# Two transformer layers on one core: q and k as two scaled fp16 parts in the two 64-row halves of the array

## What is computed

```python
x = x + _L0_attn_ref(_layernorm(x), ...)   # 16 heads of 16 dims, biases, ALiBi slopes, causal
x = x + _L0_ffn_ref(_layernorm(x), ...)    # hidden 704, int32 weights minus 128 times a scale
x = x + _L1_attn_ref(_layernorm(x), ...)   # 16 heads of 16 dims, no bias, causal
x = x + _L1_ffn_ref(_layernorm(x), ...)    # hidden 768, weights rounded to fp8
# attention, per head (layer 0 has alibi and biases):
attn = jnp.einsum('bhqd,bhkd->bhqk', q, k) / jnp.sqrt(jnp.float32(D)) + alibi
p = jax.nn.softmax(jnp.where(causal, attn, jnp.finfo(jnp.float32).min), axis=-1)
o = jnp.einsum('bhqk,bhkd->bhqd', p, v)
```

## Time and profile before

| | |
|---|---|
| median of 3 runs | 438.41 us (436.98 to 442.74) |
| profiled execution, span | 441.7 us |
| TensorE busy | 410.0 us (93%) |
| VectorE busy | 297.1 us (67%) |
| ScalarE busy | 232.9 us (53%) |
| GpSimd busy | 170.2 us (39%) |
| attention, layer 0 / layer 1 | about 37 to 168 us / 259 to 388 us |

### The profile page before, as it was taken

The page is one execution under the profiler, slowest core; times in us unless marked ns, Lnnn a source line. Parts: engine busy times, 40 slices in busy tenths (PEclk is TensorE's granted clock), DMA queues, the critical chain, the costliest instruction groups (busy, mean ns, idle before and its releaser), DMA issues.

```text
span 441.7 us, 14528 instructions
## 1 busy us (share of the span) xinstructions
PE 410.0 (93%) x6328; PEld 237.2 (54%) x6328; DVE 297.1 (67%) x596; ACT 232.9 (53%) x377; POOL 170.2 (39%) x250
## 2 busy tenths in 40 slices
PE   5799789999999988999999998998999999888997
PEld 5356564555555347544377466544555553465476
DVE  4636489999998216521336586899999981188883
ACT  3535355577776973221101541655877769635950
POOL 4107013314033144478692000234361544453770
PEclk9989799999999999999999997999999999999999
DMA  6899550000000000200100479400000000000002
GB/s 204 129 239 263 128 148 4 4 3 4 4 2 5 4 1 6 65 8 9 64 0 0 120 200 224 106 5 4 3 4 3 4 5 2 2 1 0 1 26 71
DMA packets 21657, 22.97 MB, mean 52 GB/s; under 512 B 2588, under 2 KB 20858, under 8 KB 21594
## 3 DMA queue, kind: packets, MB, share of 16 engines
q1 hardware_dynamic: 20498, 19.03, 17.8%
q0 software_dynamic: 544, 2.49, 1.9%
q10 hardware_dynamic: 552, 0.53, 0.4%
HBM read 8.27 MB, written 1.05 MB: 21 GB/s over the span
## 4 chain that ended last, share of the span: by engine, by line
PE 71%; DVE 14%; ACT 4%; DMA 3%; issue 3%; POOL 2%; SPq 2%; ACTq 0%; DVEq 0%
PE ps L785 11%; PE ps L765 11%; DVE mx L1258 11%; PE ps L743 10%; PE ps L916 8%; PE ps L1012 5%; PE ps L944 4%; PE ps L921 4%; ACT prob L1141 4%; PE ps L677 4%; PE ps L980 4%; DMA col_rows<-in_L_ffn_up_scale 3%; PE ps L845 3%; PE ps L751 2%; POOL xn L605 1%
## 5 line engine op out<-in xcount | busy, mean ns | idle before, releaser
L1258 DVE TENSOR_REDUCE mx<-ps 128x1 f32<-128x512 f32 (+3 forms) x304 | 181.1, 654 | 28.9 <-PE ps L751 24.1
L1141 ACT ACTIVATE prob<-ps 128x1024 f32<-128x1024 f32 (+1 forms) x192 | 145.4, 812 | 63.4 <-PE ps L765 63.1
L743 PE MATMUL ps<-kS,qS 96*32 96x512 bf16 (+21 forms) x1536 | 111.9, 321 | 4.4 <-DVE mx L1258 3.0
L590 POOL TENSOR_SCALAR_AFFINE_SELECT prob<-prob 128x256 f32<-128x256 f32 x128 | 51.9, 412 | 163.9 <-ACT prob L1141 162.5
L765 PE MATMUL ps<-qS,kS 101*32 101x512 bf16 (+7 forms) x1536 | 95.2, 326 | 3.7 <-ACT prob L1141 3.6
L785 PE MATMUL ps<-prob,v 128*32 128x512 f32 (+3 forms) x768 | 80.1, 489 | 0.6 <-POOL prob L590 0.4
L743 PEld LDWEIGHTS ps<-kS,qS 99*32 99x32 bf16 (+1 forms) x1536 | 42.8, 95 | 50.4 <-DVE mx L1258 28.1
L748 PE MATMUL ps<-mask_q,identb 128*32 128x32 bf16 (+1 forms) x1024 | 51.1, 186 | 2.7 <-issue 2.7
L765 PEld LDWEIGHTS ps<-qS,kS 101*32 101x32 bf16 (+1 forms) x1536 | 35.0, 96 | 31.2 <-ACT prob L1141 15.8
L751 PE MATMUL ps<-mask_q,identb 128*32 128x64 bf16 (+1 forms) x512 | 45.4, 198 | 0.0
L748 PEld LDWEIGHTS ps<-mask_q,identb 128*32 128x32 bf16 x1024 | 28.1, 98 | 14.0 <-issue 9.2
(11 more groups left out here) (146 smaller groups left out, 537.0 us busy)
## 6 DMA issues: line engine op xcount, KB each, us to landing
qS<-parts SPq DMA_DIRECT2D x24, 128.0 KB, 3.3
kS<-parts SPq DMA_DIRECT2D x24, 128.0 KB, 3.4
qS<-prob SPq DMA_DIRECT2D x12, 128.0 KB, 8.0
kS<-prob SPq DMA_DIRECT2D x12, 128.0 KB, 7.5
qS<-xn SPq DMA_DIRECT2D x12, 128.0 KB, 3.4
kS<-xn SPq DMA_DIRECT2D x12, 128.0 KB, 2.9
out<-x SPq DMA_DIRECT2D x8, 128.0 KB, 1.7
oT<-in_L_ffn_gate_w POOLq DMA_DIRECT2D x1, 768.0 KB, 4.8
```

Of the source, the lines that this page charges most:

```text
L590: nc.gpsimd.affine_select(out=square, in_=square, compare_op=ALU.is_ge, fill=0.0, base=0, pattern=[[0, 2], [1, P]], channel_multiplier=-1) ...
L743: mmi = nc.tensor.matmul(span[r:r + STRIP, 0:seen], qS[0:K_MAX[L], c, g * G + h, qt * P + r:qt * P + r + STRIP], kS[0:K_MAX[L], g * G + h, ...
L1141: nc.scalar.activation(prob[:, n % 3, 2 * pair:2 * pair + 2, off:CH], ps[:, 2 * (m % 2):2 * (m % 2) + 2, off:CH], ACT.Exp, scale=SCALE).th ...
L1258: ins = nc.vector.tensor_reduce(mx[:, slot, qt, heads[0]:heads[-1] + 1, part], src, AX_X, ALU.max)
```

## The change

- q and k are split into two fp16 parts rather than three bf16 parts. Three products of parts remain (`Q_PARTS`, `K_PARTS`), 48 rows a head; with ALiBi and the maximum 53 rows at most. Even heads stand in partitions 0 to 63, odd heads in 64 to 127 (`rows_of`), and a product is addressed to a half of the array's rows and a strip of its columns: 64 x 32 rather than 128 x 32. `mid` and its copies fall away.
- fp16 has a small range, so q and k are first scaled by powers of two `sigma` (a bound on their size from the norm of the weights: a sum of squares on ScalarE, a product with a constant on TensorE, maximum and power on GpSimd, a mask of exponent bits on VectorE). The scale goes into the weights as they are turned; the exponential's scale becomes a value in memory per partition, `exp_scale`, and was a constant. The ALiBi rows need the inverse of the scale in `qS`, written by two broadcast transfers.
- The maxima go in pairs of items: the same queries of two neighbouring heads, one in each half of the rows, into two banks of the ring of three. A diagonal item holds at most two heads (was four), so a c = 0 group has 12 items and a c = 1 group 28, in 6 and 14 pairs. `ORDER` counts pairs.
- `qS` and `kS` have half as many columns; a job is still six transfers, now of 64 KB, and each maximum is two transfers. `parts` has a slot of its own for each job and `fT` its own memory.
- Layer 1's scale is a side job (`bound_w1`) ahead of the transposes of the down weights.

```diff
-Q_PARTS = (0, 0, 0, 1, 1, 2)
-K_PARTS = (2, 0, 1, 0, 1, 0)
+Q_PARTS = (0, 0, 1)
+K_PARTS = (0, 1, 0)
...
-T_LAG = 2
-TURN_AHEAD = 5
+T_LAG = 1
+TURN_AHEAD = 3
...
+        def rows_of(h, rows):
+
+            return slice(h % 2 * HALF, h % 2 * HALF + rows)
...
+                    if (L, k) == (0, 1):
+                        sp.wait_ge(unit_row_done, 1)
+                        for half in range(2):
...
+                            sp.dma_start(q_rows[rows], src).then_inc(tail_in, 16)
...
+            def scales(L, w):
...
+                    nc.gpsimd.tensor_scalar(floored[:, L, m:m + 1], norms[:, L, m:m + 1], NORM_FLOOR[m], None, ALU.max).then_inc(sigma_step, 1)
...
+                nc.gpsimd.tensor_tensor(roots[:, L, last], floored[:, L, last], nhalf[:, last], ALU.pow).then_inc(roots_done, 1)
...
+            def bound_w0(w):
+                bank = take_a(("norm", w))
+                pe.wait_ge(squared, w + 1)
+                nc.tensor.matmul(bank[:, 0:1], to_bound[:], row_sums[:, 0, w:w + 1], start=True, stop=False)
...
+            def bound_w1():
+                bank = take_a(("norms1",))
+                pe.wait_ge(squared, 4)
+                nc.tensor.matmul(bank[:, 0:2], to_bound[:], row_sums[:, 1, :], start=True, stop=True).then_inc(a_full, 1)
...
+            def max_scores(L, n, cg, pair):
                 g, c = CGS[cg]
-                qt, part, heads, key0, keys = item
-                bank = ps[:, 4 + n % M_BANKS]
-                for i, h in enumerate(heads):
-                    span = bank[:, i * keys:(i + 1) * keys]
...
+                several = len(pair[0][2])
+                for i in range(several):
+                    for m, (qt, part, heads, key0, keys) in enumerate(pair):
+                        if i == 0 and (n + m - L * N_MAX >= M_BANKS or L):
+                            pe.wait_ge(m_free, n + m - M_BANKS + 1)
+                        span = ps[:, 4 + (n + m) % M_BANKS, i * keys:(i + 1) * keys]
+                        rows, index = rows_of(heads[i], K_MAX[L]), (g * G + heads[i]) // 2
...
                         nc.scalar.activation(prob[:, n % 3, 2 * pair:2 * pair + 2, off:CH],
-                                             ps[:, 2 * (m % 2):2 * (m % 2) + 2, off:CH], ACT.Exp, scale=SCALE).then_inc(s_free, 1)
+                                             ps[:, 2 * (m % 2):2 * (m % 2) + 2, off:CH], ACT.Exp, scale=exp_scale[:, L:L + 1]).then_inc(s_free, 1)
...
+                    act.wait_ge(w1_in, 16 * 4)
+                    for w in range(2):
+                        square_rows(1, w, w1r[:, w])
...
+            def power_of_two(L, cols):
+
+                dve.wait_ge(roots_done, 2 * L + cols.stop if L == 0 else 3)
+                nc.vector.tensor_scalar(sigma[:, L, cols].bitcast(I32), roots[:, L, cols].bitcast(I32), 0x7F800000, None,
+                                        ALU.bitwise_and).then_inc(sigma_done, 1)
...
+                    power_of_two(0, slice(0, 1))
+            power_of_two(0, slice(1, 2))
             for L in range(LAYERS):
                 if L == 0:
                     ln_normalise(0, 1)
```

402 lines of the change are left out of this document (246 added, 156 removed).

## The result

The changed kernel takes 484.6 us in the median of four runs (480.5 to 485.5) against 438.5 (437.0 to 442.7) for the kernel before on the same chip: 1.105 times its time, with a 95% interval of 1.097 to 1.112. It is slower by 46 us where I forecast 437 and a range up to 449. The profiled execution has a span of 482.6 us, against 441.7 before.

The account below looks back on a forecast made before the run. TensorE was taken to bound the c = 1 stretches, VectorE after the change. Span 441.7 - 3.6 + 1.8 + 0 + 2 - 1 = 440.9 us, scaled to the median 437.6, stated as 437 us; range 425 to 449.

Parts of the forecast that it names:

- What bounds the kernel: c = 1 stretches: TensorE fills 96% and bounds them before; after, it needs 14.3 us a group rather than 17.3.
- VectorE's limit of 16.9 us a c = 1 group: VectorE's work per c = 1 group after the change, the new bound, capping the gain at 1.2 us a group.
- The row halves: Scores in different row halves overlap, so 5.97 and 5.55 us a c = 1 group become 2.99 and 2.78.
- The rival without overlap: Halves don't overlap, a c = 1 group needs 19.7 us on TensorE: 453 us in all, chance 0.05.
- Changing the shape: Switching between scores and times v costs 0.3 us there and back, eight times a c = 1 group: 2.4 us.
- VectorE, -3.6 us: c = 1 groups take 17.5 us, with some idling on the ring of three banks: gain 0.6 us, six times.
- The VectorE-bound c = 0 groups, +1.8: Where VectorE already bound, split item, subtraction and a little idling add 0.3 us a group, six times.
- ScalarE and the ends, 0: Scale in memory adds 0.09 us per exponential, hidden in c = 1 stretches and set against idle time at attention's end.
- Start of layer 0, +2: Way to sigma and later layer 1 weights move the first exponential from 59.3 to 61.3 us.
- Start of layer 1, -1: Maxima behind the unchanged projections take half of TensorE, v jobs still between: 1 us less, bounds -4 and +3.
- the clock's rival: TensorE's work gets thin where VectorE bounds, so the clock falls; 0.7 us a step, 16 steps: 448 us, chance 0.12.

Follow-up runs that it names:

- e8: Changed kernel with both heads of a pair reading q and k from rows 0 to 63, so no score products lie in different halves: 636.6 us, 1.451.
- e5: Changed kernel with TensorE's order altered so a pair of maxima always stands between the exponential scores and times v: 478.5 us, 1.092.
- e15: Changed kernel with the maxima issued one by one between the exponential scores instead of in pairs: 467.7 us, 1.067.
- e3: Changed kernel with times v reading only the upper 16 bits as bf16, run twice, two passes instead of four: 474.1 us, 1.080.
- e9: Changed kernel with four full-array filler products ahead of every pair of maxima of groups 0 to 3: 476.2 us, 1.083.
- e4: Changed kernel with the exponentials' scale as a constant instead of a column in memory: 477.4 us, 1.079.
- e17: Changed kernel with maxima one by one, layer 1's weights one stacking job earlier and its mask after the twelfth maximum, no fillers: 460.8 us, 1.051.
- e18: The kernel of e17 with the constant scale 2 to the power -10 in the exponentials: 457.0 us, 1.041.
- e1: Changed kernel with every score product of the c = 0 groups issued twice: 481.9 us, 1.097.
- e2: Changed kernel with every score product of all groups issued twice: 507.1 us, 1.158.
- e13: Changed kernel with layer 1's weights issued one stacking job earlier and its roots masked after the sixth pair of maxima, not the ninth: 477.1 us, 1.086.
- e11: Changed kernel with layer 0's scale a constant 16, the second sum behind the turned weights and the unit-row transfers later: 485.3 us, 1.105.

## Why the prediction was wrong, point by point

**What bounds the kernel.** VectorE's limit of 16.9 us a c = 1 group was right: it is busy for 17.1. That TensorE's share would fall below it was right too. What failed there is that the gain would then be most of the distance between the two.

**The row halves.** They overlap, as the earlier trace rows said: eight products in 0.23 us, and 0.99 in e8. The rival without overlap was rightly kept small.

**Changing the shape.** 0.25 us there and back, taken at 0.3: nearly right. (In the earlier trace rows I read 0.21 from 128 x 128 to 128 x 32. The last of the eight products starts at 266.22 and L743 at 266.52, 0.09 more than the usual distance of 0.22, so that I should have said 0.2.) The Trainium skill's "TensorEngine Tiling (Array Packing)", section Tiling Modes, has it that a change of the mode drains the engine; the trace agrees, with 0.11 us in one direction and 0.14 in the other.

**VectorE, -3.6 us: wrong in sign.** I let it idle for 0.6 us a group and it idles for 1.75, so the six groups cost 5.2 us more, outside the bounds of 0 and -7.2. I had seen the mechanism (a ring of three taken in twos, times v between) and priced it at three places of 0.2 us a group. There are three waits, but they last 1.3 us together, and another 0.5 us goes in gaps too small for the view: a bank that comes free is full only 0.3 us later, the second item of a pair has to wait for its bank, and I had taken VectorE's whole stock of banks as cover for TensorE's own work. The term that was mis-sized is the price of a place. e5 (order, -0.5), e15 (pairs, -0.45) and e3 (times v, -1.0) each take part of it away.

**The VectorE-bound c = 0 groups, +1.8 (bounds +1 and +4): 18.7.** This is the step that failed most: the sum left TensorE at full clock in these stretches, and gave the case in which it is not a chance of 0.12. The only group of the six that ran wholly at full clock (the third of layer 0) takes 10.8, 0.9 more than the mean of the six before. If all did, that would be 5 us for six, a little over the bound, and by this estimate the other 13 to 14 us are the clock; e9, with the clock back in most of them and fillers to pay for, shows 7.5 of them. The rival was there, and its size was right: 0.7 us a step at the low clock was forecast, and 13.9 against 10.8 is 0.78 for each of four steps. What failed is its chance of 0.12. I took as evidence against it that from 58.5 to 86 the clock had held with TensorE waiting at times; but that was for products of 96 to 101 rows, and I carried it over to products of 48 to 53 rows without a row that says anything about them. e8 shows how far that is from being the same. I had also read the clock as a matter of gaps, and so looked for TensorE waiting; from 301.6 to 343.3 it is busy for 92% and low.

**ScalarE and the ends, 0 (bounds -2 and +3): +7.2.** The 0.09 us was exact. I set it against ScalarE's idle time in the stretch, but in a chain of exponential, scores and times v the idle time is the other engines' turn and not a reserve. About 4 us of the 7.2 are the scale (4.7 in e4, 4.0 from e17 to e18), and the rest goes with the clock: with it at 1.00 the last group takes 8.0 (e1, e2) rather than 9.3 and 10.3.

**Start of layer 0, +2: +6.2, inside the bounds of -3 and +7.** The first stacking transfer came at 19.0 (forecast 18.3) and the weights of layer 1 landed at 50.5 (forecast 47 to 51). So the weights land 5.0 us later than before, as forecast, and I let only 2 us of it reach the first exponential. They passed through nearly whole: from landing to first exponential it is 13.8 us before, 15.0 in the change and 12.7 in e13. Of what stands behind the landing e13 took away 2.3 us, the mask in VectorE's queue and the clock, which it doesn't tell apart. Of the 5.0 us by which the first stacking is later, e11 took away 2.3, with the waits for sigma and the second sum.

**Start of layer 1, -1: +3.8.** The clock again: of its four pairs of v jobs three took 3.5 to 3.7 us, where one at full clock has 2.0; before, one of the four did (3.8 us, from 273.05). That is some 3 us more. With one such pair left, with fillers the start is 1.0 over the kernel before (e9), with the maxima one by one 0.3 under it (e15).

## What to carry to other kernels

A faster engine pays only where it is the one that is waited for: here TensorE's share of a group went from 96% to well under VectorE's, and what came with the change (a ring of three taken in twos, a scale read from memory) took a little from the engines that did bound. Before packing products into parts of the array, ask what that does to the clock: look at the granted clock at the places where TensorE's work gets thin, give the clock's rival a chance as large as the stretches that it covers, and try the unpacked form with everything else kept. And follow a late transfer to its last reader through every queue, not only to its first wait.
